# Reordering SyncE's DMA queue in a fused attention and expert kernel: store of o, denominators and inverse ahead of other transfers, expert-weight pieces in other steps

## What is computed

```
# layer A, plain attention, 16 heads of 16, no mask
q, k, v = x @ Wq.T + bq, x @ Wk.T + bk, x @ Wv.T + bv
a = softmax(q k^T / 4) * head_mask
x = layernorm(x + (a v) @ Wo.T + bo)

# layer F, causal attention with rotary q and k, then a mixture of experts
r = rmsnorm(x, g1)
q, k, v = rope(r @ wq), rope(r @ wk), r @ wv
h = x + (softmax(causal(q k^T / 4)) v) @ wo
n = rmsnorm(h, g2)
w = softmax(n @ w_router); the two largest, normalised to sum 1
y = h + sum over the 2 experts of w * ((silu(n @ wg) * (n @ wu)) @ wd)   # 8 experts, hidden 704
x = layernorm(x + y)
```

## Time and profile before

| | |
|---|---|
| median of 3 executions | 1419.68 us (1417.67 to 1426.33) |
| profiled execution, in all | 1423.02 us |
| its span, first to last instruction | 1421.3 us |
| mean granted TensorE clock | 0.945 |
| TensorE busy over the span | 1259.9 us, 89% |
| VectorE, ScalarE, GpSimd busy | 67%, 58%, 55% |
| SP's DMA queue | 181.60 MB, its packets 46.6% of 16 engines' span |
| products of groups 0 to 62 leave PSUM (L1074) | 92.7 to 855.7 us |

### The profile page before, as it was taken

How to read it: one execution, slowest core, us unless ns; L and a number is a source line. 1 busy time by engine, 2 the same in 40 slices (tenths; PEclk the granted TensorE clock), 3 DMA queues, 4 the chain that set the end, 5 groups by cost and what they waited for, 6 DMA issues and landing times. The chain is left out here.

```text
span 1421.3 us, 33080 instructions
## 1 busy us (share of the span) xinstructions
PE 1259.9 (89%) x11471; PEld 693.0 (49%) x11472; DVE 959.2 (67%) x1776; ACT 823.6 (58%) x1676; POOL 778.3 (55%) x820
## 2 busy tenths in 40 slices
PE   3999999999999999999999995379999999999980
PEld 1222222322223444444444443358888888888860
DVE  7788888888897886978888736924444444444434
ACT  4078788788888776766676663134343434344434
POOL 5044465556546667576645333056666666666643
PEclk7589999999999999999999897689999999999996
DMA  6336676767767878687766433875222222223226
GB/s 183 66 78 175 184 183 188 193 186 204 199 184 215 227 220 226 206 217 200 209 165 164 115 123 126 226 210 121 42 47 42 47 44 45 42 44 48 38 27 240
DMA packets 157657, 202.53 MB, mean 143 GB/s; under 512 B 30760, under 2 KB 120616, under 8 KB 157544
## 3 DMA queue, kind: packets, MB, share of 16 engines
q1 hardware_dynamic: 140968, 181.60, 46.6%
q0 software_dynamic: 16576, 19.45, 8.6%
HBM read 110.40 MB, written 81.81 MB: 135 GB/s over the span
## 5 line engine op out<-in xcount | busy, mean ns | idle before, releaser
L1067 ACT ACTIVATE a_probs<-a_ps_s 128x512 f32<-128x512 f32 (+2 forms) x896 | 460.4, 569 | 165.1 <-PE a_ps_s L778 160.1
L1171 DVE TENSOR_REDUCE a_shift_max<-a_ps_m 128x1 f16<-128x512 f32 x512 | 320.7, 684 | 54.7 <-PE a_ps_m L783 53.4
L783 PE MATMUL a_ps_m<-a_qkx 48*128 48x128 f16 (+3 forms) x1408 | 285.2, 303 | 20.2 <-DVE a_shift_max L1171 8.7
L1868 PE MATMUL e_ps_gu<-e_xT,w_up 128*128 128x256 f16 (+1 forms) x2574 | 290.0, 269 | 4.5 <-issue 3.0
L778 PE MATMUL a_ps_s<-a_qkx 49*128 49x128 f16 (+3 forms) x1408 | 276.0, 296 | 14.3 <-ACT a_probs L1067 14.3
L1868 PEld LDWEIGHTS e_ps_gu<-e_xT,w_up 128*128 x2574 | 242.2, 98 | 38.6 <-issue 8.7
L879 PE MATMUL a_ps_o<-a_probs,a_v_one 128*32 128x512 f32 (+3 forms) x2048 | 233.8, 529 | 2.6 <-ACT a_o L1074 2.6
L778 PEld LDWEIGHTS a_ps_s<-a_qkx 49*128 49x128 f16 x1408 | 90.1, 95 | 265.4 <-ACT a_probs L1067 151.6
L1804 POOL DMA_INDIRECT h<-e_y,e_put x74 | 118.7, 1604 | 88.6 <-DVE e_y L1968 57.6
L474 POOL TENSOR_TENSOR a_o_half<-a_o_half,a_inv_half 128x512 f32<-128x512 f32 x31 | 40.0, 1289 | 222.2 <-DMA a_inv_half<-a_inv_dram 222.2
L1981 DVE TENSOR_TENSOR e_h<-e_gate,e_ps_gu 128x512 f32<-128x512 f32 (+4 forms) x156 | 79.5, 530 | 120.8 <-ACT e_gate L1931 90.2
(11 more groups left out here) (240 smaller groups left out, 1673.7 us busy)
## 6 DMA issues: line engine op xcount, KB each, us to landing
a_qkx<-a_qk_dram SPq DMA_DIRECT2D x192, 128.0 KB, 4.3
a_qk_dram<-a_qk SPq DMA_DIRECT2D x32, 512.0 KB
a_o_dram<-a_o SPq DMA_DIRECT2D x62, 256.0 KB, 2.9
part<-a_part SPq DMA_DIRECT2D x16, 512.0 KB, 5.6
a_q_swap<-a_q SPq DMA_DIRECT2D x64, 128.0 KB
a_o_half<-a_o_dram SPq DMA_DIRECT2D x31, 256.0 KB
a_inv_half<-a_inv_dram SPq DMA_DIRECT2D x31, 256.0 KB
spare<-in_wg SPq DMA_DIRECT2D x16, 352.0 KB, 5.6
```

Of the source, the lines that this page charges most:

```text
L783: return pe.matmul(out, qx[first:first + 48, r, pair, q * P:(q + 1) * P], kx[first:first + 48, r, pair, k0:k1], start=start, stop=stop)
L1067: act.activation(dst, src, ACT.Exp).then_inc(exp_out, 1)
L1171: vector.tensor_reduce(out, src, AX.X, ALU.max, negate=True).then_inc(max_out, 1)
L1868: mm = pe.matmul(ps_gu[:, bank, kind, f % 2, 0:width(r, s)], w[:, ds(e, 1)].rearrange("p o f -> p (o f)"), xT[:, s, xh, k, 0:width(r, s)], ...
```

## The change

It touches four places, and no instruction or transfer is added or taken out.

- `weights_at`: the 48 pieces are worked on in steps -4 to 31 (pieces 0 to 35) and 48 to 59 (36 to 47) instead of 0 to 47. Steps 32 to 47 have none.
- SP, even steps: `store_o` and `load_o` stand right behind `load_qk`, ahead of `store_part`, `load_res`, `load_x` and the weight pieces.
- SP, odd steps: `store_inv` is first, `load_rows` second, `load_inv` third; `store_o` and `store_x` follow.
- VectorE: `invert` runs at the end of quarter 0 of the odd step instead of quarter 1.

```diff
     def weights_at(n):
 
-        return [n] if 0 <= n < NW else []
+        if n < G * B:
+            return [n + 4] if n >= -4 else []
+        return [n - 12] if 48 <= n < NW + 12 else []
...
                 if n % 2 == 0:
                     swap((n + 6) // 2)
                     load_qk((n + 4) // 2)
+                    store_o(n - 1)
+                    load_o(n // 2 - 1)
                     if g == 0:
                         store_part(u - 3)
                         load_res(u - 1)
                     elif u + 3 > 0:
                         load_x(u + 3)
-                    store_o(n - 1)
                     for m in weights_at(n - 1):
                         store_weights(m)
                         load_weights(m + 2)
-                    load_o(n // 2 - 1)
                 else:
+                    store_inv((n - 3) // 2)
                     load_rows((n + 1) // 2)
+                    load_inv((n - 3) // 2)
                     load_last(n - 1)
                     load_last(n)
-                    store_inv((n - 3) // 2)
                     store_o(n - 1)
                     if g == 3:
                         store_x(u - 2)
-                    load_inv((n - 3) // 2)
                     for m in weights_at(n - 1):
                         store_weights(m)
                         load_weights(m + 2)
...
                         if quarter < 2:
                             rope_sum((n + 5) // 2, quarter)
-                        if quarter == 1:
+                        if quarter == 0:
                             invert((n - 3) // 2)
```

## The result

The changed kernel takes 1457.1 us (median of 4 executions, 1453.3 to 1462.3), the kernel before, on the same chip, 1418.7 (1417.3 to 1426.3). The ratio is 1.0266, 95% interval 1.0244 to 1.0289: 2.7% slower, where 0.9% faster was predicted, and outside the range. The profiled execution has a span of 1460.5 us against 1421.3. Both profiled executions are slower than their medians, by 5.2 and 4.3 us; a microsecond or two of difference between two profiles says little.

A forecast was written before the change was run, and what follows sets the result against it. In plain attention TensorE and VectorE were taken as nearly full; in the causal half TensorE waited for `aT` and `a_hid`, at times at a lowered clock. Terms summed to -12.9 us: median 1419.7 to 1406.8, range 1399 to 1418.

The forecast's parts named there:

- Inverse ahead: SP's odd steps: `load_inv` goes out 1.7 us sooner, and `normalise` comes about 2.5 us earlier.
- Passed over: `load_res`, `load_x` and `store_part` go out some 6 us later; cost 0, up to 1.5 us for `bias`.
- Three issues fewer ahead of `store_qk`, so `qkx` comes about 1 us sooner: SP without pieces in steps 32 to 47: TensorE's wait for q and k shrinks, -1.0 us, between 0 and -3.1.
- Waits for `aT`: TensorE's output projection: an earlier `normalise` removes all six waits for the low half of `aT`, -5.9 us.
- Clock: TensorE in two slow causal units: the granted clock comes back as waits go, -5.1 us, other end 0.
- Store of `o` and its denominators: SP's even steps: store to denominators takes 5 us; VectorE's waiting at the earlier reciprocal costs +0.6, upper end 4.5.
- fourth rival: VectorE stops in quarter 0 for late denominators: 1438 us if the store takes 8 us, deciding from about 7.1; 5%.
- Pieces out of 32 to 47: GpSimd goes straight from `normalise` to `part_low`, 2.6 us earlier; TensorE's waits for `a_hid` go, -4.0 us.
- Pieces into 48 to 59: GpSimd's splits there about fit before `residual` is needed: 0.5 us for each of three units, +1.5 us.
- first rival: The stall moves with the pieces to steps 48 to 59; some 9 of 12.9 us come back, 1416 us; 14%.
- GpSimd and VectorE at SBUF: Moved splits and earlier `normalise` meet other VectorE instructions: +1.0 us, between -1.5 and +1.6 for each of 12.
- Pieces into -4 to -1: Before step 0, `store_qk` and `load_qk` slip 4.6 us behind pieces, hidden by other work: cost 0.

The follow-up runs named there:

- j2: The changed kernel with the odd steps' order on SP undone, all other parts kept: 1435.6 us.
- f5: The changed kernel with the 16 KB store of the inverse issued on ScalarE's queue instead of SP's: 1442.8 us.
- k1: The kernel before with five loads of 256 bytes as a delay in `load_qk`, ahead of its six transfers: 1528.4 us.
- e3: The kernel before with the new order of the odd steps and the reciprocal in quarter 0: 1432.9 us.
- f8: The kernel before with the reciprocal in quarter 0 alone: 1434.4 us.
- j1: The changed kernel with the even steps' order on SP undone, all other parts kept: 1432.9 us.
- e1: The kernel before with the new steps of the expert-weight pieces alone: 1422.5 us.
- g1: The kernel before with every expert-weight piece four steps sooner, in steps -4 to 43: 1417.0 us.
- j3: The kernel before with the pieces in steps 0 to 31, two in each of the first sixteen: 1418.3 us.
- m1: The kernel before with the odd step's piece moved into the next even step, so none stands ahead of q and k: 1430.0 us.
- h1: The changed kernel with `store_qk` moved ahead of `load_inv` and the pieces in the odd step: 1464.6 us.
- k2: The kernel before with five loads of 256 bytes as a delay directly behind the six transfers of `load_qk`: 1441.4 us.
- f6: The changed kernel with the even step's weight piece issued behind `load_inv` in the odd step: 1458.0 us.
- f7: f6 with `x`, parts and residual of the even step also issued behind `load_inv`: 1487.6 us.
- h3: The kernel before with `store_qk` moved ahead of `load_inv` and the pieces in the odd step: 1466.7 us.

## Why the prediction was wrong

**The step that failed** is "Inverse ahead". It set `load_inv` at 317.0 instead of 318.67, 1.7 us sooner, because less stands ahead of it on SP; it took the landing of the store that `load_inv` waits for as unchanged. In the median of 27 halves the store does go out 2 us sooner (11.7 for 13.7 us after the eviction), and `load_inv` 1.6 us later (17.2 for 15.6). The 16 KB store takes 5.0 us instead of 1.5, because what was moved out of the way of `store_o` had been moved in front of it. A hint was in the step of the earlier trace rows: between 310.92 and 315.65 SP waits for the turned rows, with nothing issued but a load of 256 KB at the start, and the small store behind them had landed by 318.67, 1.4 us after its issue:

```profile
317.25 0.32 SPq L317 DMA_DIRECT2D a_inv_dram<-a_den  x1
```

The change filled that pause from both sides. "Passed over" is the same mistake: it asked only who uses `x`, the residual and `part`, and not what they stand ahead of. Its own 0 held: GpSimd's `bias` does wait for the residual in six units of the changed kernel, 28.0 us in sum, but `normalise` behind it still waits for the inverse in every half.

**"Three issues fewer ahead of `store_qk`, so `qkx` comes about 1 us sooner"**: -1.0 forecast, +18.0 measured. It holds for 16 steps only, and SP's stand at `load_inv` outweighs it: `store_qk` is 3.4 us later, `load_qk` 1.3 us. I had no row for how much later q and k may come. Of the 20.2 us of added idle time, the waits for q and k are 18.0. j2 and f5, which both leave `store_qk` nearer to where it was, take back 1.6 and 1.0 points of the 2.7%; k1 shows by itself that late q and k cost this much and more.

**Waits for `aT`**: -5.9 forecast, +4.9 measured, since `normalise` starts 1.2 us later instead of 2.5 sooner. The term was sound for an inverse that comes earlier: in e3 it does, by 2.4 us, and the waits are 0.2 us.

**Clock**: -5.1 forecast, +19.0 measured. That the clock falls behind waits of TensorE was right, and that is why it counts against this kernel: 20 us more of waiting, 19 us more of busy time for the same matmuls.

**Store of `o` and its denominators**: right. 5.1 us from store to denominators, forecast 5, and VectorE waits for none, forecast 0.6. But the sum over 29 halves that this rests on holds for the even order only. Without it (f8, e3, j1) the store to denominators takes 6.2 to 6.4 us, the same quarter 0 costs 1.1 to 1.2%, and VectorE waits 13.2 to 19.4 us, where the sum gave 4.5 for 6.3 us. The fourth rival was a real mechanism with its point of decision, 7.1 us, set too high.

**Pieces out of 32 to 47**: right in size. In e1, where the inverse is as before, the three units are 8.0 us shorter, with the part of the clock in it. **Pieces into 48 to 59**: +1.5 forecast for three units, +9.0 in e1 for two and another 4.8 for the third. The first rival, at 14%, was the likelier one for this part. It counted only the lead of `aT` over `part_low`; in e1 that lead does not exist, and a unit with pieces also has a DMA share of 0.78 where it had 0.70 without. The changed kernel shows the same: +13.8 in the two, +4.8 behind them.

**GpSimd and VectorE at SBUF**: no sign that it matters. TensorE's waits for VectorE's maxima are 9.8 us for 9.4; it was not tried by itself. **Pieces into -4 to -1**: the first product leaves PSUM at 93.9 us for 92.7, in e1 at 96.5, in g1 at 94.6, in j3, which has none there, at 90.9, but in k1 and m1, which have no pieces moved there, at 94.2 and 90.4: nothing that one profile each could tell from 0.

None of the rivals was the one that came. Two were near it, each on a part: the stall that moves with the pieces, and VectorE stopping. What stays open is how the loss divides between late q and k and late `aT`. By the stretches it is 29.9 to 11.7 us, but no run mended the one and left the other as it was (h1 and m1 did not). Why the slack of both is used up so evenly has not been looked into.

## What to carry to other kernels

When transfers are moved back in a queue, list what they now stand directly ahead of, above all small stores that something waits for; price those by their landing behind the bulk, not by the landing they have in a quiet moment. Do the same for both ends of a pause: a pause in the queue may be what makes a short transfer short. Where two chains (here q and k, and the inverse) share one queue and the kernel already shows small waits for each, put a delay of known size ahead of each of them first: here k1 and k2 would have said in two runs that neither has 3 us to spare.

## What the runs showed of the hardware

- A 16 KB store from SBUF to DRAM landed in 1.5 us in the median of the kernel before, where in most halves no large transfer was issued in the 3 us ahead of it, and in 5.0 us in the changed kernel, where in the median 1.2 MB was; 3.6 and 1.8 us with parts of that moved away (f6, f7); 5.0 us also when another engine's queue issued it (f5).
- Loads of 128 KB, issued six in a row, landed in 4.3 us each in the median (before), and in 6.3 with about 1 MB issued directly ahead of them (h3), at a DMA share of 0.70 and 0.73.
- A gap of 3.10 us in TensorE's work was followed by 10.2 us at a granted clock of 0.51; one of 4.27 us at 764.42 by 8.6 us at 0.50. Up to the last product the changed kernel has five gaps of over 3 us, with a granted clock of 0.50 to 0.68 in the 8 us behind each, and eight of 1.2 to 1.9 us, of which six left it at 1.00 and two were followed by 0.57 and 0.65.
- 3.0 us of delay of q and k in every second step cost about 3.5 us of time each.
